# Expert choice in a six-layer kernel: scores from raw X with a centred gate, choice by halves of the batches, weights split in sixteen pieces

## Chip, cores and metric

One core of a Trainium2 chip. The time is the device time of the program in microseconds: a median of timed runs, and beside it one profiled execution from which all rows are.

## What is computed

Six layers over X of shape (32, 256, 128), each adding its output to X: expert choice, RWKV, expert choice, top-2 experts, mLSTM, top-2 experts. The change is about expert choice. For each batch of 256 tokens, with layer norm without gain over 128 channels:

```python
xn = layernorm(x)                      # (T, C), T = 256, C = 128
prob = softmax(xn @ gate_w)            # (T, E), E = 8
w, tok = top_k(prob.T, 64)             # each expert takes its 64 best tokens
for e in range(8):
    y = gelu(xn[tok[e]] @ w1[e]) @ w2[e]      # 64x128 @ 128x512 @ 512x128
    out[tok[e]] += w[e] * y                    # out starts as x
```

RWKV matters too, since its loop prepares the scores of the second choice: a token-shifted mix of the normalised x, three projections, two scans over time (num and den), a sigmoid gate written as a division, an output product.

## The kernel before

X stays in SBUF as 64 tiles of 128 tokens x 128 channels, two to a batch. Five engines each run one program and meet by semaphores: PE (TensorE), ACT (ScalarE), DVE (VectorE), POOL (GpSimd), SP (DMA issue). `pipeline` (L68) writes out the first and last steps of a loop and puts those between into a hardware loop of two steps with register addresses. A step of PE, say, takes batch s in one stage and batch s-1 in the next.

*Moments.* For every batch DVE makes mean and variance (`bn_stats` L266, `bn_aggr` L272), POOL the negative mean and rstd (`Moments.rstd`, L284 to L295, with a power). At the start they come per chunk of four batches, as X lands in eight chunks.

*Scores* (L1058 to L1079). A batch is normalised into `choice_xn` (first layer: DVE, L332, after each chunk's moments; second choice: POOL, L323 and L325, in RWKV's loop), turned by two PE transposes (`turn_first`, L1065), copied from PSUM by ACT (`first_xT`, L1071), and multiplied with the gate (`score`, L1078). In RWKV's loop PE turns batch s-4 and scores s-5, and POOL normalises s-3, in the step that projects batch s. RWKV's own step: PE turns, projects (L1554, L1555) and does the output product (L1563); ACT exponentials; POOL normalises batch s+2 and adds 1 to the exponential (`er1`, L1671); DVE ekv, two scans den and num (L1624, L1626), the update of X by the batch before (L1645), under, a reciprocal (L1636), z (L1640).

*Choice* (L1264 to L1323). Softmax over all 64 tiles at once, by DVE with one exponential on ACT. PE turns the probabilities, so that a row is one (batch, expert) and 256 rows make two halves of 128. `rank` takes the 64 best of each row in eight rounds of MAX8, FIND_INDEX8, MATCH_REPLACE8, both halves in turn. Then `best_atf` and `twice` are written (L1311 to L1313), PE turns `twice`, DVE copies the slots out (L1321). SP stores the tokens to DRAM (L1455) and reads each batch's row back to all partitions (L1460).

*Gather and experts.* A group is four batches. `again` on POOL (L1417) normalises a batch once more and splits it into a rounded high part (xhi, L1423); DVE makes the rest (xlo, L1327) and the one-hot `pick` (L1334); PE gathers by matmul (L1105, L1106); ACT copies out. Four gathers precede group 0; later ones ride in the group before, one half batch per expert step. In a step PE does `up` of expert e (L1120 to L1122), `down` of e-1 (L1133 to L1135) and a gather; ACT gelu and hhi, DVE hlo (L1343). Weights are split into high (ACT, L2182) and rest (POOL, L2187), two instructions each of 128x4096, all before `again` on POOL; the first group waits for both.

Of the kernel before, what the change touches and what calls it, by code (L numbers as in the profile page):

```python
# [192 lines left out]
class Moments:  # L193
# [51 lines left out]
    def moments_first(self, dve, between=None):  # L245

        for c in range(XC):
            dve.wait_ge(self.sh.x_loaded[c], 16)
            self.take(dve, FB * c, FB, FB * c, slice(0, FB * TP), c % 2)
            if between is not None and c:  # L250
                between(c - 1)
        if between is not None:
            between(XC - 1)
# [681 lines left out]
class Choice(Layer):  # L935
# [13 lines left out]
    def __init__(self, sh, tag, w, mem):  # L949
# [13 lines left out]
        self.pick = f("pick", [P, TP, SLOTS], F32R)  # L963
        self.spread = f("spread", [P, 2, EP, T], F32R)
# [10 lines left out]
        self.max = g("max", [P, NT])  # L975
        self.sum = g("sum", [P, NT])
        self.prob = g("prob", [P, TP, B, E])
        self.ranked = g("ranked", [P, 2, 2, T])
        self.best = g("best", [P, 2, CAP])
        self.best_at = g("best_at", [P, 2, CAP], U32)  # L980
        self.best_atf = g("best_atf", [P, 2, CAP])
        self.twice = g("twice", [P, 2, 2, 2, CAP])
# [3 lines left out]
        self.pback, self.psc, self.pxt = bk[5], bk[6], bk[7]  # L986
# [9 lines left out]
        self.xa_done, self.xa_centred, self.xhi_done, self.xlo_done = s("xa_done"), s("xa_centred"), s("xhi_done"), s("xlo_done")  # L996
# [7 lines left out]
    def groups(self, eng, step):  # L1004

        pipeline(eng, step, 0, self.NGRP + 1, 2, self.NGRP - 3, self.o // self.GB)

# [50 lines left out]
    def first_norm(self, pool, b, u):  # L1058
        self.norm.gpsimd(pool, b, u, lambda: apart(pool, self.xT_ready, b - 1, self.sh.passed), self.o)

    def turn_first(self, pe, b, u):
        pe.wait_ge(self.norm.done, b + 1)
        need(pe, self.xT_done, b if self.ahead else b - 1)
        for t in range(TP):
            i = pe.transpose(self.pfirst(u)[:, t * P:(t + 1) * P], self.norm.xn[:, u, t, :], self.sh.ident[:, :])  # L1065
        i.then_inc(self.xT_ready, 1)

# [5 lines left out]
    def score(self, pe, b, u):  # L1073

        pe.wait_ge(self.xT_done, b + 1)
        for t in range(TP):
            o = self.psc[:, bass.ds(t * B * E + (b - self.o) * E, E)]
# [4 lines left out]
    def tensor(self, pe):  # L1082
        sh, w, ident, GS = self.sh, self.w, self.sh.ident, self.GS

        def turn_choice():
            pe.wait_ge(self.soft, 6 * self.run + 6)
            for h in range(2):
                for t in range(TP):
# [1256 lines left out]
```

## Time and profile before

| | us |
|---|---|
| timed runs, median of 3 (lowest, highest) | 1860.92 (1853.59, 1864.89) |
| profiled execution, its own time | 1842.0 |
| its span, first to last instruction | 1840.0 |
| PE, DVE, POOL, ACT busy | 1470.1, 1357.5, 1106.3, 1020.1 |
| mean granted TensorE clock, share of 2.4 GHz | 0.881 |

Busy shares are means over six unlike layers. The first expert choice runs from 0 to about 370 us, RWKV to about 557, the second choice to about 880. A window gives the busy time of each engine in a stretch; a timeline row gives start, length, engine, line, output and inputs, shape and count, and in brackets the idle time before it with what ended it. A row with x2 and more merges neighbours, and its length is that of all together.

### The profile page before, as it was taken

To read this page: it belongs to the slowest core of one execution; us is meant where nothing else is said; L and a number is where in the kernel's file an instruction comes from. 1 tells how busy PE (TensorE), PEld (TensorE's weight loads), DVE (VectorE), ACT (ScalarE), POOL (GpSimd) and SP (SyncE) were. 2 spreads that over 40 slices of the span, in tenths; PEclk is the share of its full clock that TensorE was granted. 3 is DMA by queue.
4 is the path that set the end of the run, shared out by engine and by line. 5 is a ranking of instruction groups with operands and counts; after the bars stand their busy time and mean duration, and the time that the engine had idled before them with its cause. 6 is when DMAs were issued, how large, how long until landed. Compare 5 with 4: busy or idle time off the path is not lost. (4 is left out here: it accounts for less than half of the span.)

```text
span 1840.0 us, 39778 instructions
## 1 busy us (share of the span) xinstructions
PE 1470.1 (80%) x10450; PEld 1350.9 (73%) x10450; DVE 1357.5 (74%) x4037; ACT 1020.1 (55%) x2524; POOL 1106.3 (60%) x1749
## 2 busy tenths in 40 slices
PE   6399999767772999999635999746999986069996
PEld 6289999756662899998514999745888875059996
DVE  7759899769996588888763777564677856447775
ACT  2288888623330888887113666513777741046764
POOL 4527787768882345543474666630598864746665
PEclk9999999979995999999667999855898976579998
DMA  5010100092000111000312222131222200122210
GB/s 183 27 44 30 35 31 24 1 221 61 0 0 19 47 36 33 31 24 2 120 51 60 65 64 55 25 89 38 82 89 73 93 1 27 55 61 64 65 52 13
DMA packets 93269, 96.18 MB, mean 52 GB/s; under 512 B 12073, under 2 KB 75710, under 8 KB 92577
## 3 DMA queue, kind: packets, MB, share of 16 engines
q1 hardware_dynamic: 83168, 76.70, 14.3%
q0 software_dynamic: 9920, 17.35, 2.8%
q8 instruction: 80, 1.31, 0.3%
q14 instruction: 101, 0.82, 0.1%
HBM read 63.75 MB, written 33.78 MB: 53 GB/s over the span
## 5 line engine op out<-in xcount | busy, mean ns | idle before, releaser
L1343 DVE TENSOR_TENSOR choice_hlo<-choice_h,choice_hhi 128x512 fp32r<-128x512 f32 x256 | 172.5, 715 | 47.0 <-ACT choice_hhi L1218 46.1
L1210 ACT ACTIVATE choice_h<-banks 128x512 f32<-128x512 f32 x256 | 152.2, 600 | 60.0 <-PE banks L1122 45.8
L795 DVE SCALAR_TENSOR_TENSOR top_h<-top_silu,top_xs,banks 128x176 f32<-128x176 f32 x364 | 128.6, 395 | 56.2 <-ACT top_silu L639 56.2
L844 POOL DMA_INDIRECT rt_rows<-X,top_slot x128 | 128.3, 1002 | 38.8 <-issue 38.8
L1120 PE MATMUL banks<-choice_xin_hi,ec_w_hi 128*128 128x256 f32 x512 | 145.7, 285 | 6.2 <-ACT choice_xin_lo L1203 4.7
L639 ACT ACTIVATE top_silu<-banks,top_xs 128x352 f32<-128x352 f32 x182 | 100.8, 554 | 88.1 <-PE banks L563 88.1
L1133 PE MATMUL banks<-choice_hhi,ec_w_hi 128*128 128x256 f32 x512 | 145.9, 285 | 3.1 <-DVE choice_hlo L1343 3.1
L1218 ACT ACTIVATE choice_hhi<-choice_h 128x512 fp32r<-128x512 f32 x256 | 146.6, 625 | 0.0
L1122 PE MATMUL banks<-choice_xin_hi,ec_w_lo 128*128 128x256 f32 x512 | 143.9, 281 | 0.0
L1121 PE MATMUL banks<-choice_xin_lo,ec_w_hi 128*128 128x256 f32 x512 | 143.8, 281 | 0.0
L1135 PE MATMUL banks<-choice_hhi,ec_w_lo 128*128 128x256 f32 x512 | 143.2, 280 | 0.0
L1134 PE MATMUL banks<-choice_hlo,ec_w_hi 128*128 128x256 f32 x512 | 143.1, 279 | 0.0
L850 POOL TENSOR_TENSOR top_y<-top_y,top_xs 128x128 f32<-128x128 f32 x182 | 82.3, 452 | 88.0 <-DVE top_y L809 87.2
L561 PE MATMUL banks<-t_w,top_xhi 128*128 x364 | 135.1, 371 | 0.0
L1429 POOL TENSOR_SCALAR choice_y_hi_lo<-choice_yw 128x512 fp32r<-128x512 f32 x64 | 41.5, 649 | 153.8 <-ACT choice_yw L1233 152.6
L581 PE MATMUL banks<-t_w,top_hhi 128*128 x364 | 129.7, 356 | 1.7 <-DVE top_y L809 1.6
L801 DVE TENSOR_TENSOR top_hlo<-banks,top_hhi 128x384 fp32r<-128x384 f32 x182 | 101.5, 558 | 37.6 <-ACT top_hhi L644 32.9
L562 PE MATMUL banks<-t_w,top_xhi 128*128 x364 | 119.1, 327 | 0.0
L563 PE MATMUL banks<-t_w,top_xlo 128*128 x364 | 118.9, 327 | 0.0
L543 PE MATMUL banks<-ident,top_xs 128*128 128x128 f32 x182 | 50.6, 278 | 81.2 <-issue 45.8
L857 POOL DMA_INDIRECT out_x<-top_y,top_xs x91 | 90.8, 997 | 34.5 <-issue 30.9
L857 POOL DMA_INDIRECT rt_y<-top_y,top_xs x91 | 90.3, 992 | 32.2 <-issue 29.7
(305 smaller groups left out, 5478.6 us busy)
## 6 DMA issues: line engine op xcount, KB each, us to landing
choice_token_row<-choice_tokens SPq DMA_DIRECT2D x64, 256.0 KB, 3.1
mlstm_run_row<-mlstm_run SPq DMA_DIRECT2D x32, 512.0 KB, 3.6
rt_rows<-rt_blank SPq DMA_DIRECT2D x2, 6188.0 KB, 35.9
top_xs<-rt_rows SPq DMA_DIRECT2D x182, 68.0 KB, 1.9
X<-in_x SPq DMA_DIRECT2D x8, 512.0 KB, 6.5
ec_stage<-in_ec_w SPq DMA_DIRECT2D x2, 2048.0 KB, 11.6
X<-rt_y SPq DMA_DIRECT2D x8, 512.0 KB, 7.0
rt_rows<-X,top_slot POOLq DMA_INDIRECT x128, 2.3
```

The lines of the kernel that those rows point to most:

```text
L561: pe.matmul(out, hi, w_hi, start=True, stop=False)
L581: pe.matmul(out[:, 0:2 * C], self.hhi[:, u % 4, k], tile[:, bass.ds(at, 2 * C)], start=(n == 0), stop=False)
L857: pool.indirect_dma_start(d.y[self.run], bass.IndirectOffsetOnAxis(ap=at, axis=0), y, None, bounds_check=NT * P - 1, oob_is_err=False).the ...
L1120: pe.matmul(o, w.w1_hi[:, e, k], hi, start=True, stop=False)
L1121: pe.matmul(o, w.w1_hi[:, e, k], lo, start=False, stop=False)
L1122: i = pe.matmul(o, w.w1_lo[:, e, k], hi, start=False, stop=True)
L1133: pe.matmul(o, w.w2_hi[:, e, c, :], self.hhi[:, ue, c, :], start=(c == 0), stop=False)
L1134: pe.matmul(o, w.w2_hi[:, e, c, :], self.hlo[:, ue, c, :], start=False, stop=False)
L1135: i = pe.matmul(o, w.w2_lo[:, e, c, :], self.hhi[:, ue, c, :], start=False, stop=(c == HC - 1))
L1210: act.activation(self.h[:, c, :], self.ph[c][:, :], ACT.Gelu).then_inc(self.gelu_done, 1)
L1218: act.activation(o, self.h[:, c, :], ACT.Copy).then_inc(self.hhi_done, 1)
L1343: dve.tensor_tensor(flat(self.hlo), self.h[:, c, :], flat(self.hhi).bitcast(F32), ALU.subtract).then_inc(self.hlo_done, 1)
```

## The change

- Scores. PE transposes X itself, as soon as its chunk has landed (first layer) or its update is done (second choice); nobody writes `choice_xn` for the scores. The gate is multiplied once by (I - 1/C) on PE, so that raw x times gate is centred; softmax multiplies by rstd before the exponential. Max is taken before that product. PE's score loop is written out.
- RWKV. POOL's `first_norm` goes; PE turns batch s-2 and scores s-3; PE's loop of 35 steps is written out in full.
- Choice by halves of 16 batches. Softmax, turning, ranking, slots and the store of the tokens exist per half, with buffers and banks of their own. First layer: half 0 is turned after score 19, its slots after score 29, half 1's softmax follows. In both layers half 1 is ranked by one round after each expert of group 0, its slots made at the first expert of group 1, and its tokens stored between rows 9 and 10 of the row reads.
- Weights. Sixteen pieces of 128x512: ACT does twelve after the copies 20 to 31, POOL two `again`, twelve pieces, two `again`, four pieces, one `again`. Group 0 waits for the first matrix only; the second is awaited before the first `down`.

Its core:

```diff
     def turn_first(self, pe, b, u):
-        pe.wait_ge(self.norm.done, b + 1)
+        k = b - self.o
+        if self.ahead:
+            pe.wait_ge(self.sh.x_done, (self.layer - 1) * B + k + 1)
+        elif k % FB == 0:
+            pe.wait_ge(self.sh.x_loaded[k // FB], 16)
         need(pe, self.xT_done, b if self.ahead else b - 1)
         for t in range(TP):
-            i = pe.transpose(self.pfirst(u)[:, t * P:(t + 1) * P], self.norm.xn[:, u, t, :], self.sh.ident[:, :])
+            i = pe.transpose(self.pfirst(u)[:, t * P:(t + 1) * P], self.sh.X[:, bass.ds(TP * k + t, 1), :].rearrange("p a c -> p (a c)"),
+                             self.sh.ident[:, :])
...
@@ Choice.tensor
         def step(g, gp):
...
+                if self.nth(g) == 0 and e == 1:
+                    w.split.ready(pe)
                 if e and self.has_group(g):
                     down(g, e - 1)
+                if self.nth(g) == 1 and e == 0:
+                    turn_slots(1)
+                if self.nth(g) == 1 and e == 1:
+                    pe.wait_ge(self.slots_done, 2 * self.run + 2)
...
         if not self.ahead:
-            self.turn_first(pe, self.o, 0)
-            pipeline(pe, first, 0, B - 1, 2, B - 3, self.o)
-        turn_choice()
-        w.ready(pe)
+            self.turn_first(pe, 0, 0)
+            self.turn_first(pe, 1, 1)
+            w.centre_gate(pe, self.psc)
+            for b in range(B):
+                if 0 < b < B - 1:
+                    self.turn_first(pe, b + 1, (b + 1) % 2)
+                self.score(pe, b, b % 2)
+                if b == self.CHOSEN_AT:
+                    turn_choice(0)
+                if b == self.SLOTS_AT:
+                    turn_slots(0)
+        else:
+            turn_choice(0)
+            turn_slots(0)
+        turn_choice(1)
...
@@ Choice.scalar
+            for b in range(B):
+                self.first_xT(act, b, b % 2)
+                if b == 0:
+                    self.w.keep_gate(act, self.psc)
+                if b == self.CHOSEN_AT:
+                    exponential(0)
+                if b > self.CHOSEN_AT:
+                    self.w.split.scalar_piece(act, next(pieces))
+            exponential(1)
...
@@ Choice.vector
+        def rank_round(h, r):
+            eight = slice(8 * r, 8 * r + 8)
+            now, later = self.ranked[h][:, r % 2, :], self.ranked[h][:, 1 - r % 2, :]
+            dve.wait_ge(self.rank_steps, ranking(h, 2 * r + 1))
+            dve.max(self.best[h][:, eight], now).then_inc(self.rank_steps, 1)
+            dve.wait_ge(self.rank_steps, ranking(h, 2 * r + 2))
+            if r < rounds - 1:
+                dve.match_replace(later, self.best[h][:, eight], now, -1.0)
+            dve.max_index(self.best_at[h][:, eight], self.best[h][:, eight], now).then_inc(self.rank_steps, 1)
...
                 if self.has_group(g):
                     hlo(g, e)
+                if self.nth(g) == 0:
+                    rank_round(1, e)
+                if self.nth(g) == 0 and e == E - 1:
+                    rank_end(1)
+                if self.nth(g) == 1 and e == 0:
+                    slots(1)
...
         if not self.layer:
-            sh.moments.moments_first(dve, lambda c: [norm(b, b % 2) for b in range(FB * c, FB * c + FB)])
-        softmax()
-        rank()
-        for h in range(2):
-            slots(h)
+            sh.moments.moments_first(dve)
+        assert rounds == E
+        softmax(0)
+        rank_begin(0)
+        for r in range(rounds):
+            rank_round(0, r)
+        rank_end(0)
+        slots(0)
+        softmax(1)
+        rank_begin(1)
...
@@ Choice.gpsimd
-        self.w.split.rest_once(pool)
-        pool.wait_ge(self.xT_ready, self.o + B)
-        for q in range(self.GB + 1):
+        pool.wait_ge(sh.moments.scaled, self.layer * B + B)
+        split, cut = self.w.split, B - 1 - self.CHOSEN_AT
+        for q in range(2):
             again(self.o + q, q % 2)
+        for i in range(0 if self.run else cut):
+            split.rest_piece(pool, i)
+        for q in range(2, self.GB):
+            again(self.o + q, q % 2)
+        for i in range(split.steps if self.run else cut, split.steps):
+            split.rest_piece(pool, i)
+        again(self.o + self.GB, 0)
...
@@ Choice.sync
-        pipeline(sp, row, 0, B - 1, 2, B - 3, self.o)
+        store(0)
+        pipeline(sp, row, 0, 9, 2, 9, self.o)
+        store(1)
+        pipeline(sp, row, 10, B - 1, 10, B - 3, self.o)
...
@@ Rwkv.tensor, step
-                self.ahead_for_next(pe, self.next.turn_first, s - 4, u)
-                self.ahead_for_next(pe, self.next.score, s - 5, 1 - u)
+                self.ahead_for_next(pe, self.next.turn_first, s - 2, u)
+                self.ahead_for_next(pe, self.next.score, s - 3, 1 - u)
...
-        self.steps(pe, step)
+        for s in range(B + 3):
+            step(s, s % 2)
...
@@ Rwkv.gpsimd, step
-            if self.next is not None:
-                self.ahead_for_next(pool, self.next.first_norm, s - 3, 1 - u)
```

## Rows read from the trace of the kernel before

**Rows 1.** Windows: stretch, length, busy (xinstructions) of PE, PEld, DVE, ACT, POOL, PEclk, DMA.
```profile
10.80:52.50 41.70, 37.77 (x187) 36.69 (x187) 30.47 (x158) 11.92 (x32) 14.46 (x20) 1.00 0.38 141
53.96:84.40 30.44, 2.49 (x8) 1.29 (x8) 25.04 (x98) 7.64 (x3) 22.05 (x10) 1.00 0.07 19
```

**Rows 2.** Timeline (start us, length us, engine, line, op), first chunks of X.
```profile
7.79 1.64 DVE L266 BATCH_NORM_STATS2 bnstats<-X 128x6 f32<-128x128 f32 x8 [0.36 <-DMA X<-in_x]
...
10.14 1.08 DVE L332 TENSOR_SCALAR choice_xn<-X,negmean,rstd 128x128 f32<-128x128 f32 x4
```

**Rows 3.** Timeline of PE, two batches of scores; L1065 by source line (ns min/median/max).
```profile
47.06 0.67 PE L1065 MATMUL banks<-ident,choice_xn 128*128 128x128 f32 x2
...
48.23 0.67 PE L1065 MATMUL banks<-ident,choice_xn 128*128 128x128 f32 x2
...
L1065 PE MATMUL banks<-ident,choice_xn x128: 272/421/477, 10.9 to 563.0; 128*128 128x128 f32 x128
```

**Rows 4.** Timeline, softmax and start of the ranking, first choice.
```profile
53.96 0.69 DVE L1273 TENSOR_REDUCE choice_c_max<-banks 128x64 f32<-128x512 f32 x1 [3.13 <-PE banks L1078]
...
55.41 0.63 ACT L1257 ACTIVATE choice_c_prob<-choice_c_prob 128x512 f32<-128x512 f32 x1 [2.58 <-DVE choice_c_prob L1275]
...
59.28 0.76 DVE L1296 COPY choice_c_ranked<-banks 128x256 f32<-128x256 f32 x2 [1.21 <-PE banks L1090]
```

**Rows 5.** Instructions of the tile ranked: ns min/median/max.
```profile
L1300 DVE MAX8 choice_c_best<-choice_c_ranked x32: 405/412/418, 60.0 to 587.1; 128x8 f32<-128x256 f32 x32
...
L1303 DVE FIND_INDEX8 choice_c_best_at<-choice_c_best,choice_c_ranked x32: 416/418/420, 60.7 to 587.8; 128x8 uint32<-128x256 f32 x32
```

**Rows 6.** Timeline, end of the ranking and first gather, first choice.
```profile
77.19 0.67 DVE L1311 CAST choice_c_best_atf<-choice_c_best_at 128x64 f32<-128x64 uint32 x1
...
79.70 0.46 DVE L1321 COPY choice_slot_token<-banks 64x64 f32<-64x64 f32 x2 [0.78 <-PE banks L1095]
...
84.42 0.88 DVE L1334 TENSOR_SCALAR choice_pick<-choice_token_row,iota_part 128x512 fp32r<-128x512 f32 x2 [2.38 <-DMA choice_token_row<-choice_tokens]
```

**Rows 7.** The weight split by source line; then timeline: xhi of again(3), first gather of group 0.
```profile
L2187 POOL TENSOR_TENSOR ec_w_lo<-ec_stage,ec_w_hi x2: 8824/8829/8834, 59.6 to 68.4; 128x4096 fp32r<-128x4096 f32 x2
...
89.41 0.41 POOL L1423 TENSOR_SCALAR choice_xhi<-choice_xn 128x256 fp32r<-128x256 f32 x1 [0.20 <-POOL choice_xn L325]
...
96.25 0.39 PE L1105 MATMUL banks<-choice_pick,choice_xhi 128*128 128x512 f32 x1
```

**Rows 8.** Group 0 of the first choice: its window, and DVE by line.
```profile
94.75:122.02 27.27, 25.43 (x196) 24.02 (x197) 15.30 (x28) 24.56 (x48) 7.18 (x12) 1.00 0.15 40
...
L1343 DVE TENSOR_TENSOR choice_hlo<-choice_h,choice_hhi 128x512 fp32r<-128x512 f32 x16 | 10.4, 691 | 12.7 <-ACT choice_hhi L1218 12.7
```

**Rows 9.** The RWKV loop: its window, and z by source line.
```profile
415.17:540.21 125.04, 98.69 (x553) 81.65 (x552) 124.67 (x255) 39.45 (x92) 107.17 (x185) 1.00 0.09 20
...
L1640 DVE TENSOR_TENSOR rwkv_z<-rwkv_num,rwkv_over x32: 424/670/841, 390.7 to 555.2; 128x256 f32<-128x256 f32 x32
```

**Rows 10.** Timeline of DVE and POOL in RWKV, steps 3, 4 and 9.
```profile
401.02 0.41 DVE L1623 TENSOR_TENSOR rwkv_ekv<-banks,rwkv_ek 128x256 f32<-128x256 f32 x1
...
405.88 0.41 DVE L1623 TENSOR_TENSOR rwkv_ekv<-banks,rwkv_ek 128x256 f32<-128x256 f32 x1
...
436.79 0.61 POOL L323 TENSOR_TENSOR rwkv_xn<-X,negmean 128x256 f32 x1 [0.16 <-issue]
...
436.88 0.81 DVE L1640 TENSOR_TENSOR rwkv_z<-rwkv_num,rwkv_over 128x256 f32<-128x256 f32 x1
```

**Rows 11.** Timeline, end of RWKV and second choice.
```profile
555.18 0.42 DVE L1640 TENSOR_TENSOR rwkv_z<-rwkv_num,rwkv_over 128x256 f32<-128x256 f32 x1
...
565.03 0.69 DVE L1273 TENSOR_REDUCE choice_c_max<-banks 128x64 f32<-128x512 f32 x1 [6.55 <-PE banks L1078]
...
588.62 0.22 DVE L1313 TENSOR_SCALAR choice_c_twice<-choice_c_best 128x128 f32<-128x128 f32 x1
...
594.05 0.88 DVE L1334 TENSOR_SCALAR choice_pick<-choice_token_row,iota_part 128x512 fp32r<-128x512 f32 x2 [1.65 <-DMA choice_token_row<-choice_tokens]
```

More of the change, by code:

```diff
@@ L1242, in step @@
                     yev(g - 1, 1 - gp, E - 1)
+                if self.nth(g) == 1 and e == 1:
+                    act.wait_ge(self.tokens_stored, 32 * (self.run + 1))
                 if e and self.has_group(g):
@@ new lines, in softmax, with link @@
+        def softmax(h):
+            before = self.SOFT * (2 * self.run + h)
+            def link(i, k):
+                i.then_inc(self.soft, 1)
+                dve.wait_ge(self.soft, before + k)
+            by = lambda t: t[:, h, :].unsqueeze(2).to_broadcast([P, NT // 2, E])
+            half = slice(h * TP * self.BH * E, (h + 1) * TP * self.BH * E)
+            score = self.pscore(h)[:, half].rearrange("p (n e) -> p n e", e=E)
+            rs = sh.moments.rs[:, h * self.BH:(h + 1) * self.BH, :].rearrange("p b t -> p (b t)")
+            logit = self.logit[:, h, :, :]
+            dve.wait_ge(self.scored, self.o + B if self.ahead else (h + 1) * self.BH)
+            dve.wait_ge(sh.moments.scaled, self.layer * B + (h + 1) * self.BH)
+            link(dve.tensor_reduce(self.max[:, h, :], score, AX.X, ALU.max), 1)
+            link(dve.tensor_tensor(logit, score, by(self.max), ALU.subtract), 2)
+            link(dve.tensor_tensor(logit, logit, rs.unsqueeze(2).to_broadcast([P, NT // 2, E]), ALU.mult), 4)
+            link(dve.tensor_reduce(self.sum[:, h, :], logit, AX.X, ALU.add), 5)
+            link(dve.reciprocal(self.max[:, h, :], self.sum[:, h, :]), 6)
+            for t in range(TP):
+                part = self.max[:, h, :].rearrange("p (b t) -> p b t", t=TP)[:, :, t].unsqueeze(2).to_broadcast([P, self.BH, E])
+                source = logit.rearrange("p (b t) e -> p b t e", t=TP)[:, :, t, :]
+                i = dve.tensor_tensor(self.prob[:, h, t, :, :], source, part, ALU.mult)
+            i.then_inc(self.soft, 1)
@@ L1541, in turn @@
             need(pe, self.x1_done, b)
-            if self.next is not None and inside(b - 6):
-                pe.wait_ge(self.next.xT_done, self.next.o + b - 5)
+            if self.next is not None and inside(b - 4):
+                pe.wait_ge(self.next.xT_done, self.next.o + b - 3)
             for t in range(TP):
@@ L2162, with __init__ @@
 class Split:
-    def __init__(self, sh, tag, parts, stage_mem, after, loads=0, splits=0):
+    def __init__(self, sh, tag, parts, stage_mem, after, loads=0, splits=0, pieces=1):
         self.sh, self.parts, self.after, self.loads, self.splits = sh, parts, after, loads, splits
@@ L2222, in build @@
                 layer = Choice(sh, "choice", choice_w, mem)
-                mem.at = layer.big
-                choice_w.split = Split(sh, "ec", choice_w.parts, mem, 0)
+                mem.at = layer.stage_at
+                choice_w.split = Split(sh, "ec", choice_w.parts, mem, 0, pieces=8)
             elif kind == "top2":
```

230 lines of the change are left out of this document (117 added, 113 removed).

## The prediction

> **What bounds the kernel now.** I read the page's 40 slices first: PE and DVE are both high nearly everywhere, with two holes of TensorE, one at 55 to 95 us and one at 565 to 595 us. They are the two expert choices. Then windows over the front, timelines inside it, and the same for RWKV and the second choice.
>
> The first layer's front has two parts. From 10.8 to 52.5 us scores are made: PE is busy 37.8 of 41.7 us and DVE 30.5 [rows 1]. A batch there costs a normalisation on DVE, two transposes and two small matmuls. Where DVE is not in the way, two batches lie 48.23 - 47.06 = 1.17 us apart on PE [rows 3]; over all 32 the pace is (52.5 - 10.8)/32 = 1.30. Scores start only after two chunks of moments [rows 2]. From 53.96 to 84.40 us PE works 2.5 of 30.4 us and DVE 25.0 [rows 1]: softmax, 17.8 us of ranking of both halves (59.28 to the cast at 77.19) [rows 4, 6], then the tokens' way over DRAM; the first pick begins at 84.42 [rows 6]. DVE sets the end of this part alone.
>
> RWKV is bound by DVE: 124.7 of 125.0 us busy over 23 steps, so 5.44 us a step [rows 9]. Early steps with the same DVE work take 405.88 - 401.02 = 4.86 us [rows 10]. The difference is not DVE work but stalls inside instructions: `z` takes 0.42 us at best, 0.67 at the median [rows 9], and where it takes 0.81 it began at 436.88, 0.09 us after a POOL normalisation of 0.61 us had begun [rows 10]. POOL is busy 107 of 125 us there.
>
> The second choice repeats the first without its scores: from the last z at 555.18 to softmax at 565.03, then 29.0 us to the first pick at 594.05 [rows 11].
>
> **The change, part by part.**
>
> *Scores from raw X.* The 32 normalisations on DVE go (the rescaling by 1/std moves into softmax), and PE may begin at the first chunk, about 5.0 us. DVE then takes 7.79 to 10.14 = 2.35 us a chunk [rows 2] and ends its moments near 7.79 + 7 x 2.35 = 24.2. PE turns two batches and the centred gate first; one more PE-ACT-PE round, which I put at 1.1 us, so the first score starts near 7.3 and score b ends at 8.0 + 1.17 b: b = 15 at 25.6, b = 19 at 30.2. The transposes keep the length they have now.
>
> *Softmax of half a bank.* 512 elements take 0.69 us and 256 about 0.38 (0.76 for two) [rows 4]. Max, subtract, rescale and sum at 0.40, exponential 0.35 (0.63 whole) with 0.2 of hand-over, reciprocal 0.3, two products 0.45: 2.9 us for half. The first half's exponential stands behind copy 19 on ACT, so that softmax ends at 30.9, and its turning on PE (0.75 with the hand-overs) at 31.7.
>
> *Ranking of one half.* Alone it can't interleave: MAX8 0.41, FIND_INDEX8 0.42 [rows 5] and a MATCH_REPLACE8 taken alike, with two value loads and the waits, I make 1.35 us a round against 2.23 for two halves (17.8/8). Seven rounds of 1.35, a last one of 0.93 and a copy of 0.45 give 10.8: end at 42.5.
>
> *Closing and slots.* Three small instructions: 0.55 us in the second choice, but here POOL splits weights beside them, and a cast took 0.67 with POOL busy [rows 6]. I take 1.4 (bounds 0.55 and 3): 44.0. Turning 0.75 and two more scores on PE 2.35: 47.2. Now softmax of half two 2.9, turning 0.75, copy 0.45, xlo 0.45: the first pick starts at 51.9. The token row needs 594.05 - 588.84 = 5.2 us from the end of closing [rows 11], so it lands at 49.2 and is covered, by 2.7 us. Gain 84.42 - 51.9 = **32.5 us** (bounds 26 and 38).
>
> *Weights in sixteen pieces.* Moved, not added. ACT: a piece is an eighth of a 128x4096 copy, under 0.6 us, with a 0.38 copy per 1.17 us; it fits. POOL: 8.83/8 = 1.10 us a piece [rows 7]. Twelve run beside the first ranking, done near 48. Four stand behind again(3) and ahead of again(4). again(3) ends at 89.82 in the rows [rows 7], here at 57.3; the pieces take it to 61.8, again(4) (two passes and a cast, 2.0 us) to 63.8, xlo and pick to 64.9. The gather that needs them began at 96.25 [rows 7], here 63.75, and it holds up the next expert by 1.2 us, of which the first wait for hlo, which falls in the same place, gives back some: **+0.9 us** (0 to 3). The split as a whole is ready at 61.8, before the first down-projection asks for it.
>
> *Second half ranked in group 0.* Eight rounds of 1.35 us on DVE. Group 0 takes 27.27 us with DVE busy 15.3 and idle 12.7 before hlo, in eight steps [rows 8]: 1.6 us of cover a step. Queued behind a round are the next xlo, pick and hlo, for which PE waits. In odd steps the cover is about 1.1 us, so some 0.25 is exposed, and ACT (24.6 of 27.3 busy) has no slack to give back. I take 1.5 us for the rounds, 0.8 for closing, 0.7 for turning and slots at the head of group 1: **+3.0 us**, twice, since both layers do it (bounds 0 and 10.8 each). SP's second store has a wait that blocks rows 10 on, which are wanted four steps later, and costs nothing.
>
> *RWKV.* POOL loses the two passes of choice_xn, about 1.4 us of every step, so its own rwkv normalisation moves ahead into DVE's long reciprocal instead of onto z. What is left to collide is er1 and the small rstd steps with the two scans. Step: not under 4.86, not over 5.44; I take 5.05. 23 steps x 0.39 = **-9.0 us** (0 and -13). On PE, turning and scoring move from four and five steps back to two and three; the turned batch was updated by DVE before the z that out(s-1) has waited for, so no new wait ends last. If it did, projections of the next batch are queued behind it.
>
> *RWKV's tail.* The last z ends at 555.60 [rows 11]. Its output product and update take about 1.8 us, the batch's transposes 0.7, the copy 0.5, the scores 0.9: 559.5; moments and rstd, beside them on DVE and POOL, about 2.5 after the update: 559.9. Softmax starts at 560.0 against 565.03 [rows 11], no longer behind normalisations queued on POOL: **-5.0 us**.
>
> *Second choice.* Softmax 2.9, turning 0.75, ranking with copy 10.8, closing 0.55, turning and slots 0.75 + 0.95 (two pairs of 0.46) [rows 6], softmax 2.9, turning 0.75, copy 0.45, xlo 0.45: 21.3 against 29.0 [rows 11]: **-7.7 us** (-5 to -9).
>
> **Sum.** -32.5 + 0.9 + 3.0 - 9.0 - 5.0 - 7.7 + 3.0 = -47.3 us. The profiled execution took 1842.0 us around a span of 1840.0; it becomes 1794.7. The median of the timed runs, 1860.92, is 19 above it and I keep that distance: **1813.6 us**.
>
> A page of the Trainium skill speaks against the pieces. "SBUF — State Buffer", section "Who interferes with whom", says that a VectorE instruction with two SBUF inputs, or in a two-port mode, and a GpSimd instruction that reads SBUF exclude each other for the whole instruction. By it each closing instruction and each such step of the second softmax could wait a piece of 1.10 us, some 3 to 5 us in all where I took 0.85. Nothing in the sum uses it.
>
> **The rivals.**
>
> *A: RWKV keeps its pace.* DVE and POOL collide at other places, or the loop's own addressing makes the steps long: the fast steps 3 and 4 are written out, the slow ones lie in a loop, and steps 3 and 4 already had choice_xn. Against it: z's row, whose long cases stand on a POOL instruction [rows 10]. Then 1813.6 + 9 = **1822.6**.
>
> *B: TensorE's clock rises during the scores.* PE would be busy without gaps from 5 us on. Transposes then shrink from 0.42 to the 0.27 us of their shortest row [rows 3], and the round over ACT sets a pace near 0.75. Softmax one starts at 24.3, when moments end, and the first pick comes some 5 us earlier: **1808.6**. Against it: at 47 us PE ran two batches back to back and the transposes still had the long form. "TensorE: Matmul & The Clock Gate" of the Trainium skill, section "Why this matters for your kernels", says that a continuously busy engine reaches 2.4 GHz, while its Part 4 says transposes don't count as busy; by the first 1808.6 holds, by the second 1813.6.
>
> *C: the ranking is only moved.* Engines in group 0 form one ring (PE up, ACT, DVE hlo, PE down) and PE is busy 25.4 of 27.3 us. If each round is exposed whole, 8 x 1.35 = 10.8 us in either choice instead of 1.5: +18.6, **1832**.
>
> *D: slower.* Mechanism: in RWKV the raw X of batch s-2 becomes part of PE's ring with DVE's update; PE waits, the projections behind it come late, and DVE, now full, idles each step. Without RWKV's gain the rest saves 38.3 us, so it decides from 38.3/32 = 1.2 us of wait a step; at 2.0 us a step the time is 1822.6 + 64 = **1887**. Against it: the order of DVE's own program, named above.
>
> **How the numbers follow.** The forecast 0.62; A 0.17; B 0.09; C 0.08; D 0.02; something unnamed 0.02. Bounds of the terms add a few us on either side, and the timed medians scatter by about 5. 1797 to 1832 holds B, the forecast, A and most of C. Every case but D and half of the unnamed lies more than 1% below before (about 19 us, near what a measurement tells from no change): faster 0.96, within 1% 0.02, slower 0.02.
>
> **What would show it.** The first pick at 51 to 53 us; PE's pace 1.17 in the scores; the ranking near 10.8 us per half; group 0 at 29 to 31 us with rounds between hlo and pick; RWKV's step near 5.05 with z near 0.42 us; softmax two at 560 on today's scale, that is about 5 us after the last z; first pick 21 us behind it. I am wrong if z stays at 0.67, if PE waits for x_done in RWKV, or if DVE idles in the front for anything but scores.

## The result, and the profile after

The changed kernel takes 1811.11 us, median of four runs (1808.79 to 1815.88), where the kernel before takes 1857.26 (1853.35 to 1864.89) in the same session: a ratio of 0.9757, with a 95% interval of 0.9728 to 0.9785, or 46 us less. The forecast was 1813.6, from a sum of -47.3 us. On two other occasions, with the same two kernels side by side, the difference was 50.7 and 46.8 us.

By stage, from the two profiles. A stage's term is its own length after less its length before.

| stage | forecast | before | after | term |
|---|---|---|---|---|
| start to first pick of the first choice | -32.5 | 84.42 | 52.89 | -31.5 |
| first pick to start of group 2 | +0.9 +3.0 | 69.87 | 74.48 | +4.6 |
| RWKV, 23 steps | -9.0 | 125.04 | 114.01 | -11.0 |
| end of last z to second choice's softmax | -5.0 | 9.43 | 4.65 | -4.8 |
| softmax to first pick, second choice | -7.7 | 29.02 | 22.47 | -6.6 |
| first pick to start of group 2 | +3.0 | 70.92 | 72.88 | +2.0 |

The rows sum to -47.3, which is the forecast's sum only because its misses of up to 2.0 us cancel; the groups and steps between them add -1.6, and the last group of the second choice starts at 775.37 against 824.31, 48.9 us earlier. The spans themselves are only 33.0 us apart (1840.0 and 1807.0). What stands between is taken up under "A loss that isn't the change's".

The front. Timelines of the changed kernel (start us, length us, engine, line, op, then idle time and its releaser); first PE, where the scores run:

```profile
6.65 1.02 PE L1098 MATMUL banks<-ec_gate,choice_xT 128*128 128x8 f32 x4 [0.27 <-ACT ec_gate L1565]
7.52 0.67 PE L1079 MATMUL banks<-ident,X 128*128 128x128 f32 x2
...
8.70 0.67 PE L1079 MATMUL banks<-ident,X 128*128 128x128 f32 x2
...
45.62 0.69 PE L1116 MATMUL banks<-ident,choice_c_twice 128*128 128x128 f32 x2 [2.65 <-DVE choice_c_twice L1368]
```

The first score begins at 6.65 instead of 11.99 (its transposes at 5.07 instead of 10.86), and two batches lie 1.18 us apart. That is the pace that [rows 3] showed, now from the first batch on. DVE and POOL, same kernel, from the end of the first ranking on:

```profile
41.54 0.43 DVE L1357 MAX8 choice_c_best<-choice_c_ranked 128x8 f32<-128x256 f32 x1
...
42.53 2.76 DVE L1366 CAST choice_c_best_atf<-choice_c_best_at 128x64 f32<-128x64 uint32 x1
...
52.89 1.23 DVE L1389 TENSOR_SCALAR choice_pick<-choice_token_row,iota_part 128x512 fp32r<-128x512 f32 x2
...
59.90 2.91 DVE L1389 TENSOR_SCALAR choice_pick<-choice_token_row,iota_part 128x512 fp32r<-128x512 f32 x2
65.96 0.82 DVE L1382 TENSOR_TENSOR choice_xlo<-choice_xn,choice_xhi 128x256 fp32r<-128x256 f32 x1 [3.15 <-POOL choice_xhi L1486]
```

```profile
35.33 9.91 POOL L2282 TENSOR_TENSOR ec_w_lo<-ec_stage,ec_w_hi 128x512 fp32r<-128x512 f32 x8
47.75 1.26 POOL L2282 TENSOR_TENSOR ec_w_lo<-ec_stage,ec_w_hi 128x512 fp32r<-128x512 f32 x1 [2.51 <-ACT ec_w_hi L2277]
...
58.23 5.73 POOL L2282 TENSOR_TENSOR ec_w_lo<-ec_stage,ec_w_hi 128x512 fp32r<-128x512 f32 x4
...
65.52 0.41 POOL L1486 TENSOR_SCALAR choice_xhi<-choice_xn 128x256 fp32r<-128x256 f32 x1 [0.20 <-POOL choice_xn L321]
```

The first pick answers to 84.42 in [rows 6]. The last of the eight rounds begins at 41.54 and the first began at 31.82, so a round is 9.72/7 = 1.39 us. Two instructions are far longer than their like: the cast that closes the ranking, 2.76 us, and the picks at 59.90, 2.91 for two, where the pair at 52.89 takes 1.23. Both lie beside POOL's pieces: eleven back to back from 31.63 to 45.24 (the row above shows the last eight), and four from 58.23 to 63.96. The rounds themselves, which lie beside the same eleven, kept their lengths: MAX8 0.43, FIND_INDEX8 0.42 and MATCH_REPLACE8 0.41 us.

Windows of the changed kernel; columns as in [rows 1]. They are the first ranking, group 0 of the first choice, the 23 steps of RWKV and group 0 of the second choice:

```profile
31.30:42.50 11.20, 11.20 (x60) 11.20 (x58) 10.58 (x39) 8.28 (x19) 11.20 (x10) 1.00 0.00 1
65.35:94.99 29.64, 28.47 (x196) 26.60 (x196) 26.19 (x66) 24.68 (x48) 9.43 (x16) 0.92 0.12 34
385.23:499.24 114.01, 98.56 (x553) 81.64 (x552) 113.60 (x255) 39.55 (x92) 82.41 (x138) 1.00 0.10 22
...
552.05:581.66 29.61, 27.78 (x196) 25.86 (x196) 24.51 (x64) 24.80 (x48) 6.88 (x12) 0.95 0.11 33
```

During the first ranking all engines work side by side, PE all the time, where before PE worked 2.5 of 30.4 us [rows 1]. In group 0 DVE went from 15.30 busy of 27.27 us [rows 8] to 26.19 of 29.64, and the granted clock from 1.00 to 0.92: its first 5.0 us (65.35 to 70.34) ran at 1.2 GHz. In RWKV the instructions of DVE are as many as before (255) and it is still always busy, but for 113.60 us instead of 124.67 [rows 9]; POOL went from 107.17 to 82.41. By line, group 0's hlo and the whole of z:

```profile
L1398 DVE TENSOR_TENSOR choice_hlo<-choice_h,choice_hhi 128x512 fp32r<-128x512 f32 x16 | 11.9, 781 | 2.6 <-ACT choice_hhi L1251 2.6
```

```profile
L1725 DVE TENSOR_TENSOR rwkv_z<-rwkv_num,rwkv_over x32: 424/424/493, 360.7 to 513.7; 128x256 f32<-128x256 f32 x32
```

DVE's idle time before hlo was 12.7 us and is 2.6: for the most part the rounds have filled it. z has a median of 0.424 us where it had 0.670 [rows 9].

### The profile page after: what moved, and what is told of

Same layout as the page of the kernel before. It is cut to its first block and busy times, and to the rows that moved or that the text cites. A ratio compares the mean times of both kernels' runs of the same rounds, so it can differ in the third digit from the quotient of the medians.

```text
span 1807.0 us, 39131 instructions
## 1 busy us (share of the span) xinstructions
PE 1473.8 (82%) x10452; PEld 1354.6 (75%) x10452; DVE 1345.3 (74%) x3991; ACT 1023.4 (57%) x2541; POOL 1074.7 (59%) x1700
## 5 line engine op out<-in xcount | busy, mean ns | idle before, releaser
L1398 DVE TENSOR_TENSOR choice_hlo<-choice_h,choice_hhi 128x512 fp32r<-128x512 f32 x256 | 177.7, 735 | 22.7 <-ACT choice_hhi L1251 22.0
L853 POOL DMA_INDIRECT out_x<-top_y,top_xs x91 | 90.8, 998 | 34.4 <-issue 31.5
L291 POOL TENSOR_TENSOR rstd<-rstd_steps,minus_half 128x2 f32<-128x2 f32 (+2 forms) x112 | 98.1, 876 | 13.7 <-POOL rstd_steps L281 9.1
```

The lines of the kernel that those rows point to most:

```text
L853: pool.indirect_dma_start(d.y[self.run], bass.IndirectOffsetOnAxis(ap=at, axis=0), y, None, bounds_check=NT * P - 1, oob_is_err=False).the ...
L1398: dve.tensor_tensor(flat(self.hlo), self.h[:, c, :], flat(self.hhi).bitcast(F32), ALU.subtract).then_inc(self.hlo_done, 1)
```

## The experiments

Twelve runs were made, on chips 0 and 11, four to a session with the kernel before beside them. There the kernel before takes 1842.69, 1840.79 and 1840.36 us (medians of seven, seven and nine).

**The kernel before, once more, and with PE's RWKV loop written out.** The first is unchanged. The second has only this edit, to test whether register addressing makes RWKV's steps long (rival A):

```diff
-        self.steps(pe, step)
+        for s in range(B + 5):
+            step(s, s % 2)
```

> The kernel before, unchanged, profiled once more. The first profiled execution took 1842.0 us, 11 us less than the lowest timed run (1853.35), and its two row dispatches of the top-2 layers took 83.9 and 80.9 us against 92.2 and 87.6 in the changed kernel. Theory: that difference of 15 us is one of executions, not of the change, so this execution takes 1853 to 1865 us and its dispatches about 90 us each, while the first expert, z of RWKV and the last group start where they did (94.8, 390.7, 824.3, each within 1 us). Rival: the change made the dispatches longer; then they stay near 84 and 81 here and the time near 1842.

> The kernel before with nothing changed but PE's program in RWKV written out for all 37 steps. Theory of POOL and DVE: the step stays at 5.44 us. Rival (register addressing of the PE loop cost time): the step falls towards 4.96 and the last z comes up to 11 us earlier than 555.6.

Measured: 1838.06 and 1843.89 us; the 23 steps take 124.62 and 124.64 us, as before. The form of the loop does nothing to the step.

**POOL normalises for nobody in RWKV.** The changed kernel, but POOL makes the two passes of `choice_xn` in RWKV as it did before; nobody reads them. Besides the lines shown only the counts of the semaphores are put right.

```diff
+            if self.next is not None:
+                self.ahead_for_next(pool, self.next.idle_norm, s - 3, 1 - u)
```

> The changed kernel, in which POOL goes on normalising one batch into choice_xn in every step of RWKV, for nobody. Theory (POOL and DVE exclude each other, and choice_xn was what pushed POOL's work onto z): RWKV's step goes back from 4.96 to about 5.44 us, z from 0.42 to about 0.67 at the median, the time up by 23 x 0.48 = 11 us. Rival (the step became short because PE's loop is written out or because PE turns raw X two steps earlier): step stays at 4.96, time within 2 us.

Measured: 1805.02 us, ratio 0.978 (0.9746 to 0.9814); the changed kernel was not run beside it and took 1790.09 and 1793.60 in later runs. The first expert starts at 65.10 (65.35 in the changed kernel); the 23 steps take 125.07 us instead of 114.01, and the last group starts 11.1 us later. z by source line:

```profile
L1733 DVE TENSOR_TENSOR rwkv_z<-rwkv_num,rwkv_over x32: 424/674/843, 359.2 to 524.3; 128x256 f32<-128x256 f32 x32
```

That is the row of before [rows 9], its median within 4 ns, with everything else of the change in place. All of RWKV's gain is POOL's two passes, and rival A is out.

**Both halves ranked in the front.** The changed kernel, with the rounds of half 1 taken out of group 0 and put behind `rank_begin(1)`; their closing stays in group 0:

```diff
-                if self.nth(g) == 0:
-                    rank_round(1, e)
...
         rank_begin(1)
+        for r in range(rounds):
+            rank_round(1, r)
```

> The changed kernel with the eight rounds of the second half taken out of group 0 and put directly behind rank_begin(1), in both layers. Each round is 1.39 us, so the first pick comes 8 x 1.39 - 0.46 = 10.7 us later in either choice. Theory (rounds hide well in group 0, which grew from 27.3 to 29.6 and from 28.4 to 29.6 us): group 0 falls back to about 27.3 and 28.4, so each layer loses 8.4 and 9.5 us, +18 us in all. In the first layer POOL's last four pieces are partly covered by the ranking, which gives some of it back. Rival C of the prediction (the ranking was only moved): within 4 us of the changed kernel.

Measured: 1810.72 us, ratio 0.9829 (0.98 to 0.9859). The first pick is at 63.54, 10.7 us later, and group 0 takes 28.83 us instead of 29.64. In the second choice softmax to pick takes 33.1 us instead of 22.5, and group 0 27.30 instead of 29.61. The last group starts 17.2 us later than in the changed kernel. Group 0 by line:

```profile
L1398 DVE TENSOR_TENSOR choice_hlo<-choice_h,choice_hhi 128x512 fp32r<-128x512 f32 x16 | 10.4, 692 | 11.2 <-ACT choice_hhi L1251 11.2
```

The cover is there again: 11.2 us idle without the rounds, 2.6 with them. How much the rounds cost group 0 can be read only where the granted clock is alike, and it isn't here: 29.64 - 28.83 = 0.8 us in the first choice, 29.61 - 27.30 = 2.3 in the second. Group 0 of the second choice without the rounds, and with them in a later run (GpSimd's closing free), both at full clock:

```profile
571.36:598.65 27.29, 25.42 (x196) 24.07 (x196) 15.28 (x30) 24.57 (x48) 6.95 (x12) 1.00 0.14 40
...
548.71:577.08 28.37, 26.49 (x197) 24.27 (x197) 24.50 (x64) 24.80 (x48) 6.89 (x12) 1.00 0.10 35
```

Eight rounds (11.1 us) cost 1.1 us. With 6 us of the group at 1.2 GHz it took 28.8 without them (first choice here) and 30.1 with them (second choice of the changed kernel on its last profile), a difference of 1.3 us. They are hidden, and rival C is out. The expectation that group 0 of the first choice would fall to 27.3 missed by 1.5 us, and the clock is the difference: 6.0 of its 28.83 us lie at 1.2 GHz, and none of the second choice's 27.30.

**The first choice waits for all scores.** Half 0's softmax begins after score 31 instead of beside scores 20 to 31. PE turns the half and its slots after the last score, and ACT makes its exponential there:

```diff
-            dve.wait_ge(self.scored, self.o + B if self.ahead else (h + 1) * self.BH)
+            dve.wait_ge(self.scored, self.o + B if self.ahead else B)
```

> The first choice waits for all 32 scores before its first softmax; everything else of the change stays (raw X, halves, second half ranked in group 0). Theory 1 (the lead of the first pick comes to a good part from choosing beside the scores 20 to 31): scores end near 44.2, and from there it takes the 22.5 us that the second choice takes from its softmax to its pick, so the first pick is at 66 to 67 instead of 53, and the time is 12 to 14 us above the changed kernel's. Theory 2 (the first half's ranking slows the scores and GpSimd's pieces slow the ranking, so that side by side gives little): first pick at 56 to 60, time 3 to 7 us above.

Measured: 1805.43 us, ratio 0.9811 (0.9796 to 0.9826), against 1793.60 for the changed kernel in that session: +11.8, just under the 12 to 14 expected. DVE's timeline:

```profile
43.64 0.42 DVE L1331 TENSOR_REDUCE choice_c_max<-banks 128x32 f32<-128x256 f32 x1 [18.73 <-PE banks L1098]
...
60.29 0.20 DVE L1365 CAST choice_c_best_atf<-choice_c_best_at 128x64 f32<-128x64 uint32 x1
...
67.10 1.24 DVE L1388 TENSOR_SCALAR choice_pick<-choice_token_row,iota_part 128x512 fp32r<-128x512 f32 x2
```

DVE stands idle for 18.73 us and the pick comes 14.1 us later: theory 1. The cast is instructive too: here POOL's pieces are over and it takes 0.20 us, so that the 14.1 us are what is left after 2.6 us won at the cast.

**DVE normalises for nobody at the start.** 64 instructions of the kernel before, on the chunks of X, with nobody to read them. My edit put those of a chunk ahead of the next chunk's moments and not behind them, so that DVE also waits for POOL's rstd at each of the eight chunks; POOL's `again` and its pieces start behind the last of them:

```diff
+            if between is not None and c:
+                between(c - 1)
             self.take(dve, FB * c, FB, FB * c, slice(0, FB * TP), c % 2)
```

> VectorE normalises X chunk by chunk at the start, as in the kernel before, but for nobody: 64 instructions of 0.27 us. TensorE still works from raw X. Theory 1 (in the front VectorE is full: moments 18.3 of 20.3 us busy before the first softmax, so each of its microseconds is on the path): moments end at 42.6 instead of 25.3, the first pick is at 68 to 70.5 instead of 53, and the time is 15 to 17.5 us above the changed kernel's. Theory 2 (TensorE's early start on raw X is what counts, VectorE's relief not): the first pick moves by less than 6 us.

Measured: 1825.02 us, ratio 0.9912 (0.9897 to 0.9927), +31.4 where 15 to 17.5 were expected. A chunk, and the first softmax:

```profile
10.21 2.14 DVE L1470 TENSOR_SCALAR choice_xn<-X,negmean,rstd 128x128 f32<-128x128 f32 x8 [2.63 <-POOL rstd L295]
12.26 1.64 DVE L266 BATCH_NORM_STATS2 bnstats<-X 128x6 f32<-128x128 f32 x8
...
62.07 0.42 DVE L1337 TENSOR_REDUCE choice_c_max<-banks 128x32 f32<-128x256 f32 x1
...
87.84 1.23 DVE L1394 TENSOR_SCALAR choice_pick<-choice_token_row,iota_part 128x512 fp32r<-128x512 f32 x2
```

The size was missed by my edit, since 8 waits of 2.6 us stand beside 8 x 2.14 = 17.1 us of work. The question is answered all the same: the first softmax starts 36.5 us later (62.07 against 25.54 in the changed kernel of that session) and the first pick comes 34.8 us later, though PE still works from raw X. Work and waits put on DVE ahead of the first softmax are on the path nearly microsecond for microsecond. How large the share of raw X in the gain is, this run doesn't say, since with its waits it is slower in the front than the kernel before (87.84 against 84.42).

**POOL's pieces.** Three edits of the changed kernel, and the changed kernel itself beside them. Left, the last four pieces stand behind again(4); right, piece 9 waits for the closing of the first ranking. The third kernel has both:

```diff
+        again(self.o + self.GB, 0)
         for i in range(split.steps if self.run else cut, split.steps):
             split.rest_piece(pool, i)
-        again(self.o + self.GB, 0)
```

```diff
         for i in range(0 if self.run else cut):
+            if i == 9:
+                pool.wait_ge(self.twice_done, 1)
             split.rest_piece(pool, i)
```

> The changed kernel itself, beside the kernel before on the same chip. In the earlier runs of this chip the kernel before took 1842 us and the changed kernel without its GpSimd edit 1805 us, 11 us of it the edit. Theory 1 (the row-by-row transfers that GpSimd starts before each expert phase take what the chip and session give, the change adds nothing to them): here the two groups of them take about 84 and 81 us as in the kernel before, and the changed kernel takes 1791 to 1796 us, a ratio of 0.972 to 0.976. Theory 2 (the 92 and 88 us in the changed kernel's first profile are the change's own): they stay at 92 and 88 us, and the time is about 1808 us.

> GpSimd makes the X operand of the first choice's batches 4 to 7 before the last four pieces of the weight split instead of behind them. Theory 1 (the pieces held back VectorE at the first group's picks, about 2 us, and with the operand that comes late at 65.5 they starve the start of group 0): the picks at 60 take the 1.2 us for two that they take elsewhere, the first expert's first matmul comes at 63 to 64 instead of 65.4, TensorE's clock doesn't fall there, and the time is 2 to 5 us below the changed kernel's. Theory 2 (what is late is moved: the pieces now run inside group 0, where VectorE has no idle time left, 26.2 of 29.6 us busy, and what is won ahead of the group is lost in it): first expert at 63 to 64, group 0 takes 31 to 32 us instead of 29.6, and the time is the changed kernel's within 1 us.

> GpSimd's ninth piece waits until VectorE has made the copies of the found indices that close the ranking. Theory 1 (the first of these copies took 2.76 us because it stood behind GpSimd's pieces): it takes 0.1 to 0.4 us, the first pick comes at 50.4 instead of 52.9, and the time is 2 to 3 us below the changed kernel's. Theory 2 (the copy is slow of its own): it stays above 2 us and nothing is won. Theory 3 (the four pieces of GpSimd that now start later run into the picks): the first pick is 2.5 us earlier, but the first expert's start is where it was, at 65.4, or later, and the time is the same.

> Both edits together. Theory 1 (two stalls of VectorE behind GpSimd's pieces, independent of each other): first pick at 50.4, first expert at 60.5 to 61.5, group 0 at 28 to 29.6 us, and 4 to 7 us below the changed kernel. Theory 2 (the pieces have to stand somewhere and block VectorE wherever they do): at most 2 us below the changed kernel, with group 0 at 31 us or more.

| kernel | us, median | first pick | first expert | group 0 | last group | ratio (95%) |
|---|---|---|---|---|---|---|
| changed | 1790.09 | 53.07 | 65.57 | 29.90 | 775.57 | 0.9728 (0.9711 to 0.9744) |
| pieces late | 1786.30 | 52.66 | 63.36 | 30.09 | 771.10 | 0.971 (0.9687 to 0.9733) |
| closing free | 1787.54 | 50.36 | 62.82 | 29.62 | 770.59 | 0.9711 (0.9692 to 0.973) |
| both | 1787.79 | 51.18 | 61.78 | 30.27 | 770.15 | 0.9703 (0.9682 to 0.9724) |

DVE with the closing free, and the fourth batch's picks with the pieces late:

```profile
42.37 0.35 DVE L1366 CAST choice_c_best_atf<-choice_c_best_at 128x64 f32<-128x64 uint32 x1
```

```profile
59.48 0.94 DVE L1389 TENSOR_SCALAR choice_pick<-choice_token_row,iota_part 128x512 fp32r<-128x512 f32 x2 [0.43 <-DMA choice_token_row<-choice_tokens]
60.71 1.50 DVE L1382 TENSOR_TENSOR choice_xlo<-choice_xn,choice_xhi 128x256 fp32r<-128x256 f32 x1 [0.29 <-POOL choice_xhi L1486]
```

The cast goes from 2.82 to 0.35 us and the picks from 2.91 to 0.94 as soon as the pieces lie elsewhere. In the kernel with both edits the cast took 1.14 us the first time, since the piece before the wait still ran until 43.48, and 0.38 in the repeat. With the pieces late, two stalls remain (xlo 1.50 and the pick behind it 1.51, with the pieces from 60.64 on) and group 0 is a little longer, but the path is shorter. Both stalls were theory 1's. By the end of group 0 the edits gain 2.0, 3.0 and 3.4 us, by the last group's start 4.5, 5.0 and 5.4. Of the rest 1.2 us of each lies in group 0 of the second choice (28.4 us against 29.6), which the closing's edit doesn't touch: the three kernels ran it at full clock throughout, the changed one with 3.3 us at 1.2 GHz. I had expected 4 to 7 for both together and had not expected that the parts would overlap. In time each edit alone gave what was expected, 3.8 us (2 to 5) and 2.6 us (2 to 3), but four runs of a kernel scatter by 4 to 8 us, so that these differences are near the noise.

The time of both is only 2.3 us lower. Its profile is that of the slowest of its four runs: from the last group on that execution lost what it had won. So it ran again, beside the changed kernel:

> The changed kernel, as the measure for the run behind it: 1788 to 1792 us if the session is like the last one.

> The kernel with both edits to GpSimd's pieces, again. Its last expert group began 5.4 us earlier than the changed kernel's, but its profiled run then lost 6 us in the stages after the rows are dispatched. Theory 1 (the loss there is chance: the granted clock in the last stages differs from run to run whatever the kernel): over five rounds it is 3 to 6 us below the changed kernel. Theory 2 (the loss belongs to the shift of the stages in time): it stays within 2 us of the changed kernel, and the profile shows the mLSTM stage at 220 us instead of 217 again.

Measured: 1793.60 us (ratio 0.9747, 0.9727 to 0.9768) and 1785.61 (0.9703, 0.968 to 0.9726), so 8.0 us where theory 1 had 3 to 6. Over both sessions, nine runs each, the means are 1792.2 and 1787.1: 5.1 us, with a standard error of 1.9, and 5.4 is what the stages say, the 1.2 us of the clock included. The mLSTM stage in windows of equal content, changed kernel, first in the session of the table and then in the repeat:

```profile
1256.70:1476.70 220.00, 210.73 (x1657) 188.58 (x1656) 161.98 (x550) 144.48 (x437) 176.11 (x303) 0.88 0.18 63
```

```profile
1256.90:1480.00 223.10, 214.92 (x1657) 193.22 (x1656) 165.25 (x550) 145.42 (x437) 174.35 (x303) 0.86 0.18 62
```

The same 1657 matmuls take 3 us more at a granted clock of 0.86 than at 0.88, in one and the same kernel. From its first `mlstm_hn` to the start of its last `mlstm_hg` the stage took 216.6 and 219.8 us in the changed kernel, and 219.9 and 221.9 in the version with both edits. I expected 220 again if the shift were to blame; it came, but the changed kernel had it as well, and the kernel before, unchanged, took 219.9 and 216.3 in its two profiles. So the stage varies without any shift. That the shift has no part at all isn't settled: from the last group's start to the end the two profiles with both edits took 1018.1 and 1021.8 us, and all others but that of the result 1011.6 to 1017.1. Each of the two is of the slowest run of its set.

## Why the prediction was right

The mechanisms came as written: DVE freed in the front, ranking behind the experts, DVE's instructions shorter in RWKV. That the number is so close is in part luck. The terms miss by +1.0, +0.7, -2.0, +0.2, +1.1 and -1.0 us and cancel, the wait ahead of group 0 has another cause than I gave, and the clock of TensorE, which cost 1.3 us in the first group 0, has no term.

**First pick, -32.5 against -31.5.** The steps came out as written where DVE was alone. Moments ended near 25 (24.2 was forecast), the first half's softmax ended at 30.6 (30.9), and a round took 1.39 us (1.35). Of the 31.5 us, the runs give 10.7 to ranking half 1 elsewhere and 14.1 to choosing beside the scores; the 6.7 that are left I put down to scores that end earlier. The parts were undone one at a time and were not shown to be additive. The steps as written sum to 51.5, not 51.9; the forecast has 0.4 us of rounding. The step that failed is the closing, mis-sized: 0.55 to 3 were the bounds, 1.4 was taken, and from the cast to the end it took 45.56 - 42.53 = 3.0, the upper bound.

"SBUF — State Buffer" of the Trainium skill, section "Who interferes with whom", says that a VectorE instruction with two SBUF inputs and a GpSimd instruction that reads SBUF exclude each other. The trace agrees for xlo, which has two: at 58.47, beside the pieces, it took 1.51 us instead of 0.42, and the two picks behind it 1.48 and 1.50 instead of 0.49 each. That is one piece for each of them. The cast waited longer, through the rest of one piece and two whole ones. In size, 3 to 5 us was my estimate by that rule; the rows give (2.76 - 0.20) for the cast, (2.91 - 0.94) for the picks and 1.1 for xlo, 5.6 us. But only the cast is one of the instructions that I had named; the second softmax stood beside no piece. Freeing the closing won 2.7 at the first pick. A piece took 1.24 us and not 1.10.

**Weights and group 0, +3.9 against +4.6.** The sum was close, its place was not. I had the gather for the next group late inside group 0. In fact the pieces held DVE itself, so that PE waited 2.1 us ahead of the group and the first expert came 12.46 us after the pick, not 10.3. Then group 0 grew by 2.4 us (1.5 and 0.8 forecast for rounds and closing), and the slots in group 1 cost 0.1, not 0.7. The rounds are 1.1 of these 2.4, by the pair at full clock above. The rest goes with the clock: before, group 0 ran at 2.4 GHz throughout (27.27 us, and 27.21 in the second profile), and with PE's loop written out, an edit far behind group 0, it had 4.2 us at 1.2 GHz and took 28.38. In the changed kernel PE stood idle for 2.1 us ahead of the group, whose first 5.0 us were at 1.2 GHz (5.6 and 3.8 in its two repeats). So most of this comes with the change and part of it by chance. It makes up for the closing, which cost nothing (27.30 us with the closing in the group, at full clock), and for the slots.

**RWKV, -9.0 against -11.0.** Mechanism right, size short. I kept a rest of 0.19 us a step over the undisturbed 4.86 for er1 and the rstd steps; the step is 4.96 (114.01/23), a rest of 0.10. The trace had a better bound than I used: z's shortest 0.424 is now its median.

**Tail and second choice, -12.7 against -11.4.** The tail is -4.8 for -5.0. Softmax to pick is 22.5 us, where I had 21.3; eight rounds of 1.39 instead of 1.35 are 0.3 of that, and the softmaxes took 3.6 and 3.2 us instead of 2.9. In the first, with POOL's passes beside it, one product took 0.68 us instead of 0.42. Group 0 cost 1.2 us there, group 1 with the slots 0.2, and the stretch from the pick to the first expert 0.5, which I had at nothing (2.0 for 3.0).

**Rival B**, a faster TensorE in the scores, fell. Transposes keep 0.67 us for two and the pace 1.18. The granted clock of 1.00 in [rows 1] says nothing here: the trace of the kernel before has its first record of the clock at 93.2 us, that of the changed kernel at 56.7, and a window ahead of the first record reads 1.00 whatever the clock was. The lengths say more. The same pair of transposes of X, in RWKV with the clock on record as 2.4 GHz, and at its end with 1.2 GHz on record:

```profile
371.76 0.38 PE L1079 MATMUL banks<-ident,X 128*128 128x128 f32 x2
...
515.23 0.63 PE L1079 MATMUL banks<-ident,X 128*128 128x128 f32 x2
```

One transpose has a median of 0.273 us in the sixty at 2.4 GHz, of 0.421 in the four at 1.2 GHz, and of 0.421 in the 64 of the score phase. So TensorE scored at 1.2 GHz, before and after, though in the changed kernel it was busy for 22.40 of 22.40 us from 7.50 on. "TensorE: Matmul & The Clock Gate" of the Trainium skill has two rules here: by "Why this matters for your kernels" a busy engine reaches 2.4 GHz, by Part 4 transposes don't count. By the lengths of the transposes the trace agrees with the second. **Rival D** did not come: the 23 steps keep DVE busy 113.60 of 114.01 us, so that it never waits for a late PE.

**A loss that isn't the change's.** The profile of the changed kernel shows 33.0 us, the timed runs 46. Waits of DVE in it (line, waited for: us in total, times, longest):

```profile
DVE top_n L743 <- remote: 23.3, 2, 11.6
...
DVE top_d L758 <- remote: 6.9, 2, 3.8
```

and the tile of the rows dispatched, of the changed kernel on its first chip and on chip 11:

```profile
L840 POOL DMA_INDIRECT rt_rows<-X,top_slot x128: 956/962/3934, 849.6 to 1588.8; - x128
...
  DVE top_slot L766: 15.3, 2
```

```profile
L840 POOL DMA_INDIRECT rt_rows<-X,top_slot x128: 954/959/3864, 850.6 to 1568.9; - x128
...
  issue: 38.8, 128
```

DVE stands 11.6 us in each of the two dispatches for a releaser that the trace calls "remote", and POOL's row transfers then wait 15.3 us for its slots. Between the first and the last row transfer the run took 739.2 us, on chip 11 718.3. None of the other thirteen profiles has a "remote" wait on DVE. From the last group's start to the end this profile takes 1031.6 us, the others 1011.6 to 1021.8. The first session of experiments showed all four kernels without it, and my expectation that the kernel before would come back at 1853 to 1865 was wrong. In the session of the result the kernel before took 1857 us as well, against 1841 elsewhere, and the changed one 1811 against 1790. So something of 15 to 21 us bears on both kernels, which is why the ratio holds (0.9757, 0.9728 and 0.9747). That it is this wait in the timed runs too is likely and not shown. My choice to keep 19 us between profile and median rested on no row, and that 1813.6 came so close is luck. The changed kernel's profile took 1808.79 us and not 1794.7, the median stands 2.3 above it and not 19, and in the other two sessions the same kernel took 1790.09 and 1793.60. What holds in all three is the difference, 46 to 51 us.

## What to carry to other kernels

An engine that sets a stage alone gains most when its work is laid beside another engine's long stage, here the ranking beside scores and beside experts: find where it idles per step and compare one round with that gap. Work taken from a partner engine can shorten instructions of the bounding one at an unchanged count, so look at min and median of one line before pricing it. When elementwise work on GpSimd is cut into pieces and issued back to back, an instruction of VectorE can still lose a whole piece, and one here lost more than two: put a wait or other work between the pieces where VectorE has a short instruction on the path. Before a stage's length is compared between two kernels, compare the granted clock in it: here it moved group 0 by as much as the ranking did.

## What the runs showed of the hardware that I had not expected

- Of VectorE's instructions beside back-to-back pieces on GpSimd (1.24 us each) some are not touched, some lose one piece, one loses more. Eight rounds of ranking ran beside eleven pieces at their usual lengths. A cast of 0.20 us that began at 42.53, within the same run of pieces, ended only at 45.30, when the run did. Beside four pieces an xlo and two picks took 1.51, 1.48 and 1.50 us in turn (0.42 and 0.49 elsewhere), and the pieces 1.44 to 1.47: there the two engines took turns.
- A granted clock of 1.00 at the start of a trace can be the lack of a record. In all fourteen profiles the first record comes between 54 and 105 us, and ahead of it gathers take 0.63 us, as they do where 1.2 GHz is on record; where 2.4 GHz is, they take 0.39. So all mean clocks here, the 0.881 of the kernel before too, count the front as full speed and are too high.
- TensorE's stretch before the first expert had gathers of 0.63 us from 53.4 on, then 0.40 from 56.4 on; after 2.1 us without work (from 59.3 to 61.4) they took 0.63 again, and the granted clock read 0.50 (1.2 GHz) from 60.1 to 70.3. With the closing free the matmuls had the long form until 66.2, where the first record of 2.4 GHz begins.
- Group 0 in all fourteen profiles, both choices, with the time ahead of the first record counted at 1.2 GHz by the lengths there: without rounds 27.2 to 27.3 us with no time at 1.2 GHz, 28.4 with 4.2 to 4.3 us at it, 28.8 to 29.1 with 6.0 to 6.2. With rounds 28.4 with none, 29.6 to 29.9 with 3.0 to 5.6 us, 30.1 to 30.2 with 6.0 to 6.2. The two first choices with both edits fall out of this order (30.2 and 30.3 with 3.6 and 3.7 us); pieces run inside group 0 there.
